# Attention output split into two halves in token order and turned by DMA; null probabilities turned by DMA; squares moved to ScalarE; new slot tables

## What is computed

```python
q = l2norm(xn @ Wq) * q_scale;  k, v = split(x @ Wkv);  k = l2norm(k) * k_scale
k = concat([null_k, k]);  v = concat([null_v, v])          # two null keys for each head
sim = einsum('bhid,bhjd->bhij', q, k) * 8 + slopes * -distance
sim = where(causal, -max, sim)
attn = softmax(sim)
out = einsum('bhij,bhjd->bhid', attn, v)                    # [tokens, 64] of each head
return out @ Wout                                           # summed over all heads
```

## Time and profile before

| | |
|---|---|
| Time, median of 3 runs | 3038.81 us (3033.42 to 3042.46) |
| Profiled execution | span 3041.3 us; the profile gives no other time of its own |
| PE busy | 2821.4 us (93%) |
| DVE busy | 2666.3 us (88%) |
| POOL busy | 2330.5 us (77%) |
| ACT busy | 2117.3 us (70%) |
| DMA queue of SP | 26.1% of 16 engines' span |
| Mean granted TensorE clock | 0.985 of full speed |

### The profile page before, as it was taken

How to read it: one execution, slowest core, us unless ns; L and a number is a source line. 1 busy time by engine, 2 the same in 40 slices (tenths; PEclk the granted TensorE clock), 3 DMA queues, 4 the chain that set the end, 5 groups by cost and what they waited for, 6 DMA issues and landing times. The chain is left out here.

```text
span 3041.3 us, 84128 instructions
## 1 busy us (share of the span) xinstructions
PE 2821.4 (93%) x31759; PEld 1647.2 (54%) x31759; DVE 2666.3 (88%) x6386; ACT 2117.3 (70%) x3380; POOL 2330.5 (77%) x2588
## 2 busy tenths in 40 slices
PE   3589999999999999999999999999999999999998
PEld 3245555555555555555555555555555555555554
DVE  6678989889999899898998899988998988989886
ACT  2467767776776767777777777777677776676775
POOL 5886687976789677886869768797678966788663
PEclk8799999999999999999999999999999999999999
DMA  4111232312332133222333123231233213332121
GB/s 148 44 27 35 58 71 60 70 31 67 72 73 50 31 76 67 72 42 43 77 62 78 35 56 74 61 72 31 67 72 70 54 31 67 77 67 47 33 35 42
DMA packets 457537, 178.17 MB, mean 59 GB/s; under 512 B 421552, under 2 KB 423600, under 8 KB 457136
## 3 DMA queue, kind: packets, MB, share of 16 engines
q1 hardware_dynamic: 455664, 172.69, 26.1%
q10 hardware_dynamic: 1472, 0.09, 0.0%
HBM read 55.23 MB, written 16.78 MB: 24 GB/s over the span
## 5 line engine op out<-in xcount | busy, mean ns | idle before, releaser
L1022 DVE CUSTOM_DVE_ANT_0 PS<-PS,STR 128x512 f32<-128x512 f32 (+3 forms) x1536 | 822.3, 576 | 118.3 <-PE PS L1262 116.5
L563 ACT ACTIVATE AR<-PS,SC 128x1024 f32<-128x1024 f32 (+1 forms) x640 | 658.3, 1029 | 325.5 <-PE PS L1270 152.3
L1214 PE MATMUL PS<-WH,XT 128*128 128x388 f16 x2048 | 678.1, 331 | 88.0 <-DVE AR L1029 77.8
L1217 PE MATMUL PS<-WL,XT 128*128 128x388 f16 x2048 | 678.4, 331 | 0.0
L1218 PE MATMUL PS<-WH,XT 128*128 128x388 f16 x2048 | 677.7, 331 | 0.0
L789 POOL TENSOR_TENSOR RN<-SS,HALF 128x8 f32<-128x8 f32 x256 | 428.6, 1674 | 302.6 <-DVE SS L1104 295.5
L567 ACT ACTIVATE AR<-AR 128x1024 f16<-128x1024 f32 (+1 forms) x640 | 621.8, 972 | 20.4 <-ACT AR L563 0.2
L1056 DVE TENSOR_TENSOR AR<-AR 128x768 f16<-128x768 f32 (+1 forms) x448 | 593.9, 1329 | 15.6 <-ACT AR L567 14.7
L1239 PE MATMUL PS<-AR 64*128 64x512 f16 (+3 forms) x4608 | 498.6, 325 | 4.7 <-ACT AR L563 4.5
L1287 PE MATMUL PS<-AR 128*128 128x66 f16 x4608 | 474.9, 193 | 10.6 <-POOL AR L772 10.5
L1289 PE MATMUL PS<-AR 128*128 128x64 f16 x4608 | 474.5, 194 | 0.0
(11 more groups left out here) (241 smaller groups left out, 5613.0 us busy)
## 6 DMA issues: line engine op xcount, KB each, us to landing
XW<-in_L_attn_x SPq DMA_DIRECT2D x112, 256.0 KB, 2.8
out<-ACC SPq DMA_DIRECT2D x64, 256.0 KB, 2.1
ACC<-in_L_attn_x SPq DMA_DIRECT2D x56, 256.0 KB, 2.9
AR<-QKB SPq DMA_TRANSPOSE x512, 2.5
AR<-in_L_attn_Wkv SPq DMA_DIRECT2D x2, 1536.0 KB, 13.8
ACC<-in_L_attn_x SPq DMA_DIRECT2D x2, 1024.0 KB, 7.4
AR<-in_L_attn_Wout SPq DMA_DIRECT2D x1, 2048.0 KB, 9.1
AR<-CTK SPq DMA_TRANSPOSE x128, 2.4
```

Source lines behind the costliest of these rows:

```text
L563: e.activation(PR[:, n % 2, :, 0:wide], SB[:, :, 0:wide], ACT.Exp, scale=SIG).then_inc(s_p, 1)
L1022: e.tensor_tensor_reduce(out=r[:, 0:n], in0=r[:, 0:n], in1=ST[:, u % 2, h, o:o + n], scale=1.0, scalar=LOW, op0=ALU.add, op1=ALU.max, accu ...
L1214: e.matmul(PJ, XT[:, k, xs], WH[:, k, p, :], start=k == 0, stop=False)
L1217: e.matmul(PJ, XT[:, k, xs], WL[:, k, p, :], start=False, stop=False)
```

## The change

- **Output**: ACT now rounds `OTOK`, still in token order and in SBUF, to the high half `OTK[:, 0]` (L563 of after); POOL makes the low half (L778 of after) in place of DVE; one DMA_TRANSPOSE of 128 x 1024 f16 on SP turns both halves into `OT` (`W_OTT`, L447 of after). The four f32 transposes on PE go, and so does their bank of the ring.
- **Null probabilities**: one DMA_TRANSPOSE of 128 x 256 on SP (`W_NTT`, L440 of after) takes the place of the transpose on PE and of the two copies on ACT, and the columns of `PNX` are laid out for it.
- **Squares**: ACT, function Square (L556 of after), in place of POOL.
- **Tables**: all `W_` tables and `HOLD` have new numbers. Only some are shown.

```diff
+W_OTS = [109, 145]
+W_OTL = [110, 149]
+W_OTT = [115, 152]
+W_NTT = [87, 121]
-W_PIECE = [45, 46, 48, 57, 64, 66, 70, 74, 77, 82, 84, 91]
-W_MAX = [46, 49, 52, 57, 63, 64, 69, 74, 82, 82, 84, 91]
+W_PIECE = [46, 47, 53, 58, 64, 67, 69, 74, 80, 83, 87, 89]
+W_MAX = [48, 50, 55, 59, 60, 61, 66, 70, 80, 80, 83, 91]
@@ ring_order
-        for u, qc in due(s, W_NTP):
-            take(s + HOLD[3], "nt", u, qc)
-        for u, qc in due(s, W_OTP):
-            take(s + HOLD[4], "otp", u, qc)
@@ sync
+                for u, qc in due(s, W_NTT):
+                    w.wait_ge(s_nl, 2 * u + qc + 1)
+                    if u:
+                        w.wait_ge(s_o, 2 * (2 * (u - 1) + qc) + 2)
+                    e.dma_start_transpose(PNT[:, qc, :, :], PNX[:, qc, 0:256]).then_inc(s_nt[qc], 16)
+                for u, qc in due(s, W_OTT):
+                    w.wait_ge(s_otl, 2 * u + qc + 1)
+                    w.wait_ge(s_oth, 2 * u + qc + 1)
+                    odd = u - 2 + (u + 1) % 2
+                    if odd > 0:
+                        w.wait_ge(s_op, NT * (odd // 2) + 4 * qc + 4)
+                    e.dma_start_transpose(OT[:, u % 2, qc, :, :].rearrange("p j (q n) -> p (j q) n", n=P),
+                                          OTK[:, :, :, :].rearrange("p j q n -> p (j q n)")).then_inc(s_ot[qc], 16)
@@ scalar
-                for u, qc in due(s, W_NT):
-                    w.wait_ge(s_ntp, 2 * u + qc + 1)
-                    if u:
-                        w.wait_ge(s_o, 2 * (2 * (u - 1) + qc) + 2)
-                    for h in range(2):
-                        hs = slice(64 * h, 64 * h + 64)
-                        e.activation(PNT[hs, qc, h, :], rb("nt", u, qc).bitcast(F16)[hs, 0:P], ACT.Copy).then_inc(s_nt, 1)
+                for u, g in due(s, W_SQ):
+                    i = 4 * u + g
+                    w.wait_ge(s_kvev, 4 * i + 3)
+                    if i > 1:
+                        w.wait_ge(s_ss, 2 * i - 3)
+                        w.wait_ge(s_hi, i - 1)
+                        w.wait_ge(s_lo, i - 1)
+                    e.activation(SQ2[:, i % 2, :].rearrange("p (t c) -> p t c", t=2), QKB[:, i % 3, :, 0:256], ACT.Square).then_inc(s_sq, 1)
                 for u, qc in due(s, W_OTS):
-                    w.wait_ge(s_otp, 2 * u + qc + 1)
-                    odd = u - 2 + (u + 1) % 2
-                    if odd > 0:
-                        w.wait_ge(s_op, NT * (odd // 2) + 4 * qc + 4)
-                    e.activation(OTH[:, u % 2, 512 * qc:512 * qc + 512], rb("otp", u, qc)[:, :], ACT.Copy).then_inc(s_ot, 1)
+                    i = 2 * u + qc
+                    w.wait_ge(s_on, i + 1)
+                    if i:
+                        old = i - 1
+                        w.wait_ge(s_ot[old % 2], 16 * (old // 2 + 1))
+                    e.activation(OTK[:, 0, :, :], OTOK[:, :, :], ACT.Copy).then_inc(s_oth, 1)
@@ gpsimd
-                for u, g in due(s, W_SQ):
...
+                for u, qc in due(s, W_OTL):
+                    w.wait_ge(s_oth, 2 * u + qc + 1)
+                    e.tensor_tensor(OTK[:, 1, :, :], OTOK[:, :, :], OTK[:, 0, :, :], ALU.subtract).then_inc(s_otl, 1)
@@ vector
-                for u, qc in due(s, W_OTL):
-                    w.wait_ge(s_ot, 2 * u + qc + 1)
-                    cs = slice(512 * qc, 512 * qc + 512)
-                    e.tensor_tensor(OTL[:, u % 2, cs], rb("otp", u, qc)[:, :], OTH[:, u % 2, cs], ALU.subtract).then_inc(s_otl, 1)
@@ tensor
-                for u, qc in due(s, W_NTP):
-                    r = rb("nt", u, qc).bitcast(F16)
-                    bank_free(w, "nt", u, qc)
-                    w.wait_ge(s_nl, 2 * u + qc + 1)
-                    e.transpose(r[:, 0:P], PNX[:, qc, :], IDH[:, :]).then_inc(s_ntp, 1)
-                for u, qc in due(s, W_OTP):
-                    r = rb("otp", u, qc)
-                    bank_free(w, "otp", u, qc)
-                    w.wait_ge(s_on, 2 * u + qc + 1)
-                    for q in range(4):
-                        ins = e.transpose(r[:, P * q:P * q + P], OTOK[:, q, :], IDF[:, :])
-                    ins.then_inc(s_otp, 1)
```

More of the change, by code:

```diff
@@ L62 @@
[L62 to L71, removed]
-W_SHIFT = [69, 91]
[L73 to L81, removed]
@@ new lines @@
+W_MAX = [48, 50, 55, 59, 60, 61, 66, 70, 80, 80, 83, 91]
+W_SCORE = [89, 95, 101, 105, 110, 115, 118, 128, 130, 135]
+W_PLOW = [97, 101, 101, 107, 114, 115, 127, 132, 132, 137]
+W_VALUE = [102, 109, 109, 115, 123, 128, 133, 135, 138, 138]
+W_ON = [107, 145]
+W_OTS = [109, 145]
+W_OTL = [110, 149]
+W_OTT = [115, 152]
+W_OP = [119, 125, 137, 144, 157, 158, 163, 171]
+W_ADD = [114, 126, 141, 146, 155, 155, 161, 166]
+W_PROJ = [z for z in [1, 7, 15, 25, 29, 33, 40, 42] for k in range(KC)]
+W_KV = [5, 8, 21, 24, 30, 34, 41, 47]
@@ new lines @@
+W_VL = [3, 8, 17, 21, 23, 32, 42, 48]
+W_STRIP = [30, 42]
+W_SQ = [11, 27, 41, 50]
+W_SS = [13, 21, 42, 51]
+W_POW = [24, 35, 46, 57]
+W_TP = [26, 41, 57, 72]
+W_HI = [28, 37, 54, 65]
+W_LO = [28, 36, 58, 63]
+W_ROWS = [66, 93]
+W_SHIFT = [69, 91]
+W_CTP = [74, 91]
+W_NX = [75, 105]
+W_NL = [78, 113]
+W_NTT = [87, 121]
+W_XA = [-272, -235, -159, -151, -134, -105, -96, -95]
+W_STAT = [-167, -158, -142, -127, -106, -95, -88, -88]
+W_XB = [-83, -62, -29, -23, -14, 6, 12, 22]
+W_XF = [-57, -51, -19, -1, 0, 8, 18, 31]
@@ L96 @@
+W_XH = [-43, -24, -11, 0, 3, 14, 24, 36]
+W_XL = [-38, -24, -9, 3, 5, 23, 34, 45]
+W_XTP = [-25, -23, -19, -1, 15, 22, 33, 38]
+W_SMALL = [-77, -74, -71, -54, -53]
+W_VSC = [-27]
+W_BASE = [72, 85, 99, 103, 109, 115, 142, 175]
+W_BN = [81, 88, 103, 110, 121, 135, 149, 184]
+W_BM = [86, 92, 109, 110, 121, 135, 153, 186]
+W_BA = [91, 98, 109, 114, 133, 141, 158, 186]
+HOLD = [6.1, 7.1, 7.8]
 LATE_ACT = [0, 1, 5, 6, 9, 10, 15, 16, 18, 24, 25, 27, 32, 33, 38, 39]
@@ L181, in fused_block @@
         OTF = sb("OT", [P, 2, N], F32)
-        OTH = OTF[:, 0, :].bitcast(F16).rearrange("p (j n) -> p j n", j=2)
-        OTL = OTF[:, 1, :].bitcast(F16).rearrange("p (j n) -> p j n", j=2)
+        OT = OTF[:, :, :].rearrange("p a n -> p (a n)").bitcast(F16).rearrange("p (u c j n) -> p u c j n", u=2, c=2, j=2)
         OTOK = sb("OTOK", [P, 4, P], F32)
+        OTK = sb("OTK", [P, 2, 4, P], F16)
         DS = sb("DS", [P, N], BF16)
@@ L321, in fused_block @@
         s_na, s_nx, s_nh, s_nl = (mk("s_" + z) for z in ("na", "nx", "nh", "nl"))
-        s_ntp, s_nt, s_st, s_p, s_ph, s_pl, s_plp = (mk("s_" + z) for z in ("ntp", "nt", "st", "p", "ph", "pl", "plp"))
+        s_st, s_p, s_ph, s_pl, s_plp = (mk("s_" + z) for z in ("st", "p", "ph", "pl", "plp"))
+        s_nt = [mk("s_nt0"), mk("s_nt1")]
         s_av, s_o, s_rl, s_on = (mk("s_" + z) for z in ("av", "o", "rl", "on"))
-        s_otp, s_ot, s_otl, s_op, s_add = (mk("s_" + z) for z in ("otp", "ot", "otl", "op", "add"))
+        s_oth, s_otl, s_op, s_add = (mk("s_" + z) for z in ("oth", "otl", "op", "add"))
+        s_ot = [mk("s_ot0"), mk("s_ot1")]
         s_base, s_bn, s_wo, s_wop, s_vsc = (mk("s_" + z) for z in ("base", "bn", "wo", "wop", "vsc"))
@@ L339, in bank_free @@
                 e.wait_ge(s_mx, 24 * u + i + 1)
-            elif what == "op":
+            else:
                 e.wait_ge(s_add, NT * (u // 2) + i + 1)
[L342 to L345, removed]
         class Once:
@@ L625, in _ @@
             e.memset(VNT[:, :, :], 0.0).then_inc(s_vz, 1)
-            for I in (IDF, IDH):
-                pc(e.memset(I[:, :], 0.0))
-                ins = e.affine_select(out=I[:, :], in_=I[:, :], compare_op=ALU.not_equal, fill=1.0, base=0,
-                                      pattern=[[-1, P]], channel_multiplier=1)
-                if I is IDF:
-                    pc(ins)
-                else:
-                    ins.then_inc(s_id, 1)
+            pc(e.memset(IDF[:, :], 0.0))
+            e.affine_select(out=IDF[:, :], in_=IDF[:, :], compare_op=ALU.not_equal, fill=1.0, base=0,
+                            pattern=[[-1, P]], channel_multiplier=1).then_inc(s_id, 1)
             pc(e.memset(HALF[:, :], -0.5))
```

54 lines of the change are left out of this document (13 added, 41 removed).

## The result

The changed kernel takes 2935.65 us, the median of four runs (2933.4 to 2941.35); the kernel before, run beside it, takes 3040.64 (3033.42 to 3043.64). The ratio is 0.967, with a 95% interval of 0.9653 to 0.9688. The forecast was 2938, the range 2880 to 3000.

A forecast was written before the change was run, and what follows sets the result against it. The prediction took PE as the bound of most units, with POOL and DVE costing it time in others. Its sum was 3041.3 - 70 - 35 - 25 + 20 + 5 + 3, said as 2938 us, range 2880 to 3000.

The forecast's parts named there:

- What bounds the kernel: Whole kernel: PE bounds most units; POOL and DVE take turns costing it two microseconds in the others.
- PE's transposes, -70: Output and null transposes leave PE: 68 us by distances between starts, 74 with their waits, counted as 70.
- POOL's squares, -35: Squares leave POOL, so DVE reaches `PJ` earlier and PE waits less: between nothing and 74 us, half taken, 35.
- The ring, -25: PE's ring of three banks: fewer uses and more slots before reuse return at most 51 us, 25 taken.
- ACT's work, +20: Added squares, less null copies, give ACT net +97 us; idle time covers most, so 20 us reach the span.
- SP and the transposes, +5: Added DMA transposes on SP may delay q and k for PE: between 0 and 157 us, 5 taken.
- The bar of 30 us: Sign of a wrong prediction: PE waits for q and k transposes over 30 us in total.
- The two other signs of being wrong: DVE's fullest windows above 96%, or ACT waiting for output transposes more than 0.8 us for each half unit.
- The tail, +3: Kernel's end, where nothing covers the new output chain: 4.8 us in place of 2.1.
- DVE, 2580 expected: DVE's busy time in the profile after: about 2580 us, with L1087's 87 us gone.
- DVE takes over: Rival, chance 0.20: DVE's fullest windows set the rate of all units, about 2961 to 2971 us.
- The slower rival: Chance 0.09: ACT's next output copy waits for the transpose before it to land, stopping what follows; 3130 us.

The follow-up runs named there:

- experiment 4: Changed kernel with 128 groups of four f32 transposes of a constant, for which nothing waits, put back on PE: 2972.4 us, ratio 0.978.
- experiment 3: Changed kernel with the squares back on POOL, its new tables kept: 3048.3 us, ratio 1.0031.
- experiment 6: Kernel before with only the squares moved to ACT, at four earlier slots, other tables kept: 2981.2 us, ratio 0.9815.
- Experiment 8: Changed kernel with each of the 128 output transposes issued a second time by SP, into a spare tile: 2950.4 us, ratio 0.971.
- experiment 7: Changed kernel with one table number changed (W_LO[2] from 58 to 54), one low half of q and k four slots earlier: 2927.7 us, ratio 0.9635.
- experiment 1: Changed code with all the slot tables of the kernel before: 3476.1 us, ratio 1.145.
- experiment 2: Kernel before with the changed kernel's tables, PE's transposes at the nearest slots: 3277.9 us, ratio 1.081.
- experiment 9: Changed code with the tables of the kernel before, but ACT's squares at earlier slots: 3200.5 us, ratio 1.054.
- experiment 5: Changed kernel with the output's low half on DVE in place of POOL, at three successively earlier places: 3152.6, 3121.7 and 2986.4 us.
- Experiment 5's second kernel: Changed kernel with the output's low half on DVE at slots 109 and 147, in place of 110 and 149: 3121.7 us, ratio 1.0275.

## Why the prediction was right, point by point

**What bounds the kernel.** PE, with DVE and POOL behind it: experiment 4 confirms it, since work on PE costs 0.65 of its time even in the changed kernel, and experiment 3 shows that a late DVE costs PE its time through the ring.

**PE's transposes, -70.** Right, and the choice of distances between starts was the right one: busy time fell by 72.5. The line in the part on the profile after, "near 2821 - 111 = 2710 us", was wrong, and it contradicted the sum: the page counts overlapping matmuls once, so its total falls by distances too, not by the groups' sum. But 70 was taken as if all of it came back. By experiment 4 a third of such time is swallowed by waits; counted that way the transposes gave about 45, an estimate from that one run.

**POOL's squares, -35.** The mechanism was right, the size too small. Moved alone they gave 57 (experiment 6), with the new tables 112 (experiment 3). I had halved the term because DVE would find ACT in front of it. It does: its wait for L542 is 232 us now. But little of it reaches PE: from 200 us on PE waits 5.9 us for L1025 in all. Of the 77.8 us at `PJ`, which were the upper bound of the term, 36.7 lie before 200 us, of which 7.6 came back; of the 41.1 behind, 35.2 did. And the squares also act at the ring, where the prediction gave them nothing.

**The ring, -25.** PE's waits for the maxima fell by 31 us (50.6 to 19.7). Experiment 6 took 17.5 of these 31 back (50.6 to 33.1) with the old tables and with all eight transposes in the ring, so an earlier DVE did more there than fewer uses. PE's wait for the copies of the null probabilities in the ring, 5.8 us, went as well; the prediction left it out. The term had the right size for a reason that was only in part the right one.

**ACT's work, +20.** The row of L542 gave the price well, 623 ns against 625. PE's wait for the exps is 5.3 us (4.5 before) and DVE's for the squares 7.2, so the term was too large. In experiment 6, with the old tables, the squares cost PE 12.6 us at the exps.

**SP and the transposes, +5.** Mis-sized. The waits of PE for transposes rose by 24.5 + 9.3 = 34 us. The bar of 30 us, above which I called the prediction wrong, was passed by 1.9. Experiment 8 shows that the time of the issues isn't the cause (0.12 us each), and experiment 7 that one slot is: 30.5 us of that kind of wait, some 8 of them net. The two other signs of being wrong did not come: DVE's fullest window is below 96% (at most 43.2 of 46 us, 94%), and ACT does not wait for the landing of an output transpose at all.

**The tail, +3.** From the end of L1042 (2915.95) to the issue takes 2 us and to landing 3.1 more, so 5.1 against 4.8. The term is part of the 9.3 us above: one of these waits, 4.8 us, is this one.

**DVE, 2580 expected, 2428 measured.** This failed: DVE was costed by its instruction count alone. 87 us went with the low half, but 134 came from L1056 (593.9 to 510.4 us) and L1036 (270.6 to 220.2), whose instructions became shorter (below). The rival "DVE takes over" took it that PE is held where DVE is fullest. DVE's fullest window of 46 us, in steps of half a window, holds 42.2 now, near the 42.5 expected (43.2 wherever it is laid), but PE has 45.9 in it:

```profile
1461.00:1507.00 46.00, 45.89 (x520) 25.85 (x517) 42.19 (x103) 35.99 (x58) 32.20 (x36) 1.00 0.59 100
```

That rival's time had a slip too: from 46 to 44.6 is 1.4 us a unit and not 1.25, so by its own rule it stood at about 2951 and not at 2961 to 2971.

**The sum.** With the measured sizes it reads: busy time -72.5, PE's idle time -37.3. Of the idle time -43 at `PJ`, -31 at the ring and +34 at the transposes and the tail make -40; some 12 us of waits in front of and behind PE's transposes went too, and as much in small ones came. My terms for waits, -35 - 25 + 20 + 5 + 3, make -32. Squares, ring and ACT were too cautious by 8, 6 and 20 us, the transposes with the tail too hopeful by 26. The experiments split the gain otherwise, with the same end: the removed work gives about 45 in place of 70, the squares 57 in place of 35. Either way errors of 22 to 34 us cancelled: that the forecast came within 3 us is luck.

**What was not seen.** I treated the new tables as a term of 25 us for the ring. Experiments 1, 2 and 9 show that code and tables gain only together, with one exception: for the squares alone four new slots were enough (experiment 6). The squares on ACT (276 us, experiments 1 and 9) and the low half of `OTK` (166, experiment 5) each cost more at the wrong slot than the whole change gains. The slower rival ("the single buffer holds ACT", 3130) named the right place, the chain of `OTK`, and experiment 5 produced it at 3152; but it is SP (591.0 us) and then PE (139.3) that stand; ACT waits 15.8 us for the landing.

## What to carry to other kernels

Price work that leaves a full engine by the distance between starts, and expect less than all of it back (two thirds in the one case that was tried). Where work moves to another engine in a kernel with a written-out order, read when its result is due before how long it takes: the same 128 subtractions three to four slots later cost 166 us here, though they ran for 88 us in all there and for 117 at the earlier slots. A wait that comes back at a fixed period points to one entry of a table, and moving that entry is the cheapest trial there is; read what grew beside what fell.

## What the runs showed of the hardware that was not expected

**DVE's subtractions are slower beside POOL.** One instruction of DVE, 128x512 with two f32 sources from SBUF, in the kernel before (the first row) and after (the second): minimum, median and maximum in ns.

```profile
L1036 DVE TENSOR_TENSOR QKB<-SQ,QKB x256: 673/894/2083, 103.2 to 2986.2; 128x512 f16<-128x512 f32 x128
```

```profile
L1032 DVE TENSOR_TENSOR QKB<-SQ,QKB x256: 656/686/1747, 103.5 to 2872.2; 128x512 f16<-128x512 f32 x128
```

The cause can be read from the timelines, and the place shown in experiment 7 is an example: POOL's L797 ends at 995.74 + 1.04 = 996.78, DVE's low half, which began at 996.05, ends at 996.05 + 1.27 = 997.32, that is 0.54 us later. It is so each time. In before 144 of the 256 instructions of L1036 last longer than 0.72 us, in after 92 of L1032, and every one of them ends 0.53 to 0.56 us after the end of a POOL instruction that was at work when it began. With POOL idle from its start to its end it takes 0.68 us in both kernels (40 cases before, 35 after, from 300 to 2800 us). So DVE stands until POOL's instruction is over, and pays what was left of it. Not every instruction of POOL does this: 23 times in after the low half lies wholly within L785, the power of 128x8, and takes 0.68 us. Those of DVE that read PSUM (L1029 to L1025, 345 and 347 ns in the mean) did not change.

L1056, whose sources lie in SBUF too, went from 1215 to 959 ns in the median. What decides is thus which long instruction of POOL is at work when DVE begins, and that is set by the order as well as by the amount of POOL's work. Experiment 3, with the squares back on POOL and the new tables, has L1032's successor at 830 ns in the mean (860 in after) and that of L1056 at 1218 (1155 in after, where 1329 was expected); experiment 6, with the squares off POOL and the old tables, has 1099 and 1280, against 1057 and 1329 in before. A kernel that was built to separate the two was not run.

**A long wait of PE can take its clock with it.** Experiment 5's second kernel at one of its waits, in the timeline of PE:

```profile
1534.30 0.38 PE L1301 MATMUL PS<-WO,OT 128*128 128x512 f16 x1 [3.35 <-DMA OT<-OTK]
...
1535.76 0.53 PE L1207 MATMUL PS<-WH,XT 128*128 128x388 f16 x1
...
1539.14 0.33 PE L1211 MATMUL PS<-WH,XT 128*128 128x388 f16 x1
```

And in windows (length, PE's busy us, then the granted clock, DMA share, GB/s):

```profile
1533.00:1535.00 2.00, 0.70 (x4) 1.00 0.91 189
1535.40:1538.60 3.20, 3.20 (x12) 0.50 0.40 59
1540.00:1544.00 4.00, 4.00 (x40) 1.00 0.26 64
```

After 3.35 us without work PE runs at 1.00 for 1 us more, then for 3.2 us at 0.50, the 1.2 GHz level, though it is full, and then at 2.4 GHz again. The projections start 0.32 us apart in place of 0.16, so this wait of 3.35 us costs 1.6 more. The changed kernel shows the same at its end, behind the wait of 4.85 us for the last output. But not every such wait is followed by it: at 2277.65 in experiment 5's second kernel PE has waited 3.35 us too, goes on with the same instructions, and the clock stays at 1.00. The rows of these two, the changed kernel first:

```profile
2921.40:2924.40 3.00, 3.00 (x8) 0.50 0.00 0
```

```profile
2279.00:2282.00 3.00, 3.00 (x40) 1.00 0.56 51
```

What sets the two apart was not tried. The slower versions of the changed kernel have more busy time for the same instructions, beside a lower mean clock: a mean clock of 0.939 and 2897.1 us busy in experiment 1, 0.964 and 2811.1 in experiment 5's second kernel, 0.985 and 2748.9 in the changed kernel. The prediction had no term for it, and needed none, since the mean clock is 0.985 before and after. The Trainium skill, "TensorE: Matmul & The Clock Gate", part 1 on the clock gate, describes a gate that sets TensorE's clock by how busy the engine has been of late, with 1.2 and 2.4 GHz as its two levels. The trace agrees in the levels, 0.50 and 1.00, and in these rows the lower one stands behind idle time.
